# Perceiver block on one core: the place of the expert loop's preparation in the last rounds of a hand-ordered pipeline

## The chip, the core and the metric

The kernel is one program on one core of a Trainium2 chip. The metric is the device time of one execution in microseconds (us), the median over several executions; one further execution was taken with the hardware profiler, and all rows of the trace come from that one.

## What is computed

The reference is one block of a network with batch 128, 32 rows of 512 numbers in each batch entry, and a context of 257 rows for each entry. Everything is float32.

```python
x = x + xattn(layernorm(x), ctx_1024, ...)    # self attention, cross attention to the context, relu layer
x = x + attn(layernorm(x), W_attn, W_proj)    # 16 heads, causal, softmax times a decay matrix
x = x + ffn(layernorm(x), index_b, index_t, ...)
```

The last line is the one that matters here. `ffn` gives every row a gated feed-forward ("shared") result. The rows that `index_b`, `index_t` name get, besides, the result of one of eight experts:

```python
sh = ln(silu(x @ sw1.T + sb1) * (x @ sw2.T + sb2)); shared_out = sh @ sw3.T + sb3
x_moe = x[index_b, index_t]
expert_scores = sigmoid(x_moe @ eg_w.T + eg_b);  top1_idx = argmax(expert_scores + exp_bias)
z = ln(silu(x_moe @ ew1[e].T + eb1) * (x_moe @ ew2[e].T + eb2))       # for every expert e
final_out = shared_out.at[index_b, index_t].set(shared_moe_out + expert_moe_out)
```

## The kernel before, in words

**Tiles and stages.** 4096 rows are cut into 32 tiles of 128 rows. A tile goes through some forty named units on each engine (PE, DVE, ACT, POOL, and SP for transfers): `project_out` ends the head attention and gives x2, the rows that enter the feed-forward part; `x2_norm` normalizes them; `turn_x2n`, `ffn_in`, `ffn_in_l` are the transposes and the first product; DVE's `ffn_in` adds the bias, ACT's `ffn_in` is a tanh, `silu` and `z_norm` make the gated, normalized row; `turn_z`, `ffn_out`, `ffn_out_l` transpose and multiply it; DVE's `ffn_out` adds bias and x2, and SP stores the rows. Products are split in a float16 high part (line 1453) and a remainder (line 1462). What PE needs between these steps is written by ACT (lines 688, 696) and POOL (584).

**What sets the order.** Each engine runs its instructions strictly in the order in which the program issues them, and that order is written out by hand. `run_pipeline` goes through 37 rounds; in each it walks the engine's list of (lag, unit), and a unit of lag g works in round n on tile n - g. Three sets of lists exist: FIRST, ORDER and, for rounds 30 to 36, LAST. Between engines only semaphores order the work. In LAST there are also `keep_clock` units, which multiply the identity matrix into a bank that nobody reads (line 1594) and act on tile 31 alone.

**After the tiles** comes the expert loop. A list of the tiles with named rows is made from the indices; the loop runs once for each such tile (here once). Every turn reads the tile's x2 back from a scratch in HBM, normalizes it, transposes it (`turn_expert_rows`), multiplies it with the 9 gate columns (`gate_logits`), and for each of 8 experts does: product to 512 columns (`expert_in(k)`, line 1587), bias (line 1270), silu (line 796), norm, scaling by the choice (line 1304), transposes (line 1646) and the second product (line 1655). DVE begins a turn with a short chain on the logits, lines 1273 to 1291, which yields the coefficients, and only then adds the bias of expert 0.

**The units of this change.** The preparation for the loop's first turn stands in the pipeline, and acts on tile 31 alone:

```python
def first_rows(s, r, tile):            # DVE
    if tile == FINAL:
        dve.wait_ge(e_x2_loaded, 16)   # x2 of the first listed tile is back from HBM
        expert_moments(step, x2[:])    # lines 1215 to 1218
        dve.wait_ge(e_rstd_ready, 1)   # from POOL, line 600
        nc.vector.tensor_scalar(e_xn[:], x2[:], ...).then_inc(xn_ready, 1)   # line 1233
def first_rows(s, r, tile):            # PE: transposes (line 1575), then the gate products (line 1581)
        turn_expert_rows(1); gate_logits(1)
def first_expert(s, r, tile):          # PE: expert 0's first product (line 1587)
        expert_in(0)
```

ACT's `first_rows` copies the transposed rows out of PSUM (line 775), between PE's two steps; POOL's is the power that gives 1/std (line 600). On SP, `store_x2` (line 460) writes a tile's x2 to the scratch, and `first_x2` (line 508) waits until the stores of all tiles have landed and then reads the first listed tile. SP's list is the same in both kernels.

Of the kernel before, what the change touches and what calls it, by code (L numbers as in the profile page):

```python
# [121 lines left out]
        (2, "turn_x2n"), (1, "out_norm"), (1, "turn_x1n")],  # L122
}
LAST = {
    "pe": [(3, "ffn_out"), (3, "ffn_out_l"), (3, "first_rows"), (3, "first_expert"), (2, "project_q_l"),
        (1, "context_mix"), (2, "head_scores"), (2, "keep_clock0"), (0, "turn_xn"), (2, "project_v"),
        (0, "project_self"), (1, "turn_w"), (1, "keep_clock4"), (0, "project_self_l"), (1, "context_out"),
        (1, "keep_clock5"), (2, "project_v_l"), (2, "keep_clock2"), (0, "self_scores"), (0, "value_self"),
        (0, "value_self_l"), (0, "turn_p"), (2, "head_mix"), (2, "keep_clock1"), (1, "turn_h2"), (0, "self_mix"),
        (2, "project_out"), (2, "project_out_l"), (2, "keep_clock3"), (1, "hidden"), (1, "hidden_l"), (0, "turn_h"),  # L130
        (2, "turn_x2n"), (2, "keep_clock6"), (0, "project_query"), (0, "project_query_l"), (2, "ffn_in"),
        (0, "context_scores"), (2, "ffn_in_l"), (2, "keep_clock7"), (1, "turn_x1n"), (1, "project_k"),
        (1, "project_q"), (2, "turn_z"), (1, "project_k_l"), (0, "turn_pc")],
    "dve": [(3, "x2_norm"), (2, "hidden"), (2, "out_norm"), (2, "x1_norm"), (3, "ffn_in"), (3, "silu"),
        (1, "context_scores"), (3, "z_norm"), (3, "first_rows"), (2, "project_k"), (3, "ffn_out"), (0, "xn_moments"),
        (0, "turn_xn"), (2, "head_scores"), (1, "context_mix"), (1, "context_total"), (2, "head_total"),
        (2, "head_weights"), (0, "project_self"), (1, "context_out"), (0, "self_scores"), (1, "context_norm"),
        (0, "self_mix"), (2, "project_out"), (0, "self_norm")],
    "act": [(3, "turn_x2n_t"), (2, "turn_x1n"), (3, "ffn_in"), (2, "turn_x1n_t"), (1, "context_scores"),
        (3, "turn_z"), (3, "turn_z_t"), (3, "first_rows"), (1, "turn_pc"), (2, "project_k"), (2, "project_q"),  # L140
        (0, "turn_xn"), (0, "turn_xn_t"), (2, "head_scores"), (1, "turn_w"), (2, "project_v"), (0, "self_scores"),
        (0, "value_self"), (0, "turn_p"), (2, "head_mix"), (2, "head_mix_t"), (1, "turn_h2_t"), (1, "turn_h2"),
        (0, "turn_h"), (0, "turn_h_t"), (2, "turn_x2n"), (0, "project_query")],
    "pool": [(3, "silu"), (3, "first_rows"), (3, "turn_z"), (0, "xn_moments"), (0, "turn_xn"), (2, "head_scores"),
        (1, "context_out"), (2, "head_mix"), (0, "self_mix"), (1, "turn_h2"), (2, "project_out"), (0, "turn_h"),
        (1, "hidden"), (2, "turn_x2n"), (1, "out_norm"), (1, "turn_x1n")],
}
# [1581 lines left out]
```

## Time and profile before

| | |
|---|---|
| median of 3 runs | 1496.43 us (1494.0 to 1496.84) |
| the profiled execution | 1495.49 us, of which span 1493.6 us |
| mean granted TensorE clock | 0.987 of full speed |
| busy: PE, DVE, ACT, POOL | 1401.0, 1101.4, 530.6, 480.4 us |

The span is the time from the first to the last instruction of the trace; 1.9 us lie around it. The busy share is an average: the part that the change touches is the last 70 us of the span, in which tiles 30 and 31 drain out of the pipeline and the loop follows.

### The profile page before, as it was taken

To read this page: it belongs to the slowest core of one execution; us is meant where nothing else is said; L and a number is where in the kernel's file an instruction comes from. 1 tells how busy PE (TensorE), PEld (TensorE's weight loads), DVE (VectorE), ACT (ScalarE), POOL (GpSimd) and SP (SyncE) were. 2 spreads that over 40 slices of the span, in tenths; PEclk is the share of its full clock that TensorE was granted. 3 is DMA by queue.
4 is the path that set the end of the run, shared out by engine and by line. 5 is a ranking of instruction groups with operands and counts; after the bars stand their busy time and mean duration, and the time that the engine had idled before them with its cause. 6 is when DMAs were issued, how large, how long until landed. Compare 5 with 4: busy or idle time off the path is not lost.

```text
span 1493.6 us, 32437 instructions
## 1 busy us (share of the span) xinstructions
PE 1401.0 (94%) x13668; PEld 883.8 (59%) x13668; DVE 1101.4 (74%) x2215; ACT 530.6 (36%) x979; POOL 480.4 (32%) x499
## 2 busy tenths in 40 slices
PE   7779999999999999999999999999999999999789
PEld 3346666666565666666666566666656666665444
DVE  6667777777777777787777777777777777777645
ACT  2533333334333333333333333333433333343221
POOL 0033333333333333333333333333333333333211
PEclk9899999999999999999999999999999999999899
DMA  9632344333233344433323234444323324434530
GB/s 349 251 119 79 135 142 142 142 141 125 96 129 110 110 142 142 142 142 137 107 109 131 97 131 142 142 142 142 130 97 123 117 104 142 142 135 163 190 108 22
DMA packets 38657, 201.37 MB, mean 135 GB/s; under 512 B 5096, under 2 KB 5992, under 8 KB 28400
## 3 DMA queue, kind: packets, MB, share of 16 engines
q1 hardware_dynamic: 37792, 199.19, 37.2%
q8 instruction: 108, 1.77, 0.5%
q14 instruction: 37, 0.30, 0.1%
q10 hardware_dynamic: 720, 0.10, 0.0%
HBM read 182.24 MB, written 17.04 MB: 133 GB/s over the span
## 4 chain that ended last, share of the span: by engine, by line
PE 60%; DVE 22%; issue 9%; POOL 4%; ACT 3%; DMA 1%; SPq 0%; DVEq 0%; POOLq 0%; ACTq 0%
PE ps_a L1476 8%; PE ps_a L1442 8%; PE ps_t L1476 7%; PE ps_t L1434 6%; DVE stats L1005 4%; PE ps_a L1453 4%; PE ps_a L1517 4%; PE ps_a L1488 4%; POOL rstd L575 4%; PE ps_t L1453 4%; PE ps_v L1453 3%; DVE kbd L1126 3%; PE ps_a L1462 2%; PE ps_t L1488 2%; PE ps_a L1498 2%
## 5 line engine op out<-in xcount | busy, mean ns | idle before, releaser
L575 POOL TENSOR_TENSOR rstd<-var,mhalf 128x1 f32<-128x1 f32 x224 | 183.9, 821 | 444.2 <-DVE var L1007 444.0
L584 POOL TENSOR_TENSOR act_l<-act_t,act_h 128x512 f16<-128x512 f32 (+1 forms) x154 | 171.1, 1111 | 349.6 <-ACT act_t L696 261.1
L688 ACT ACTIVATE act_h<-ps_t,scale 128x512 f16<-128x512 f32 (+1 forms) x110 | 71.1, 646 | 176.7 <-PE ps_t L1434 176.7
L584 POOL TENSOR_TENSOR last_slot<-last_slot 128x512 f16<-128x512 f32 (+1 forms) x70 | 77.4, 1106 | 153.6 <-ACT last_slot L696 114.1
L1126 DVE TENSOR_SCALAR kbd<-ps_a,unscale 32x512 f32<-32x512 f32 x64 | 48.2, 754 | 54.9 <-PE ps_a L1488 53.8
L1442 PE MATMUL ps_a<-wcv,act_t 128*128 128x512 f32 x176 | 82.1, 610 | 2.2 <-ACT act_t L702 2.2
L1005 DVE BATCH_NORM_STATS2 stats<-rows 128x6 f32<-128x512 f32 x110 | 76.4, 695 | 3.8
L1434 PE MATMUL ps_t<-ident,rows 128*128 128x128 f32 x352 | 57.4, 286 | 19.7 <-DVE rows L1011 19.5
L696 ACT ACTIVATE act_t<-ps_t,scale 128x512 f32<-128x512 f32 (+1 forms) x110 | 70.3, 639 | 0.2 <-PE ps_t L1434 0.2
L1453 PE MATMUL ps_a<-w_parts,act_h 128*128 128x512 f16 x264 | 65.0, 383 | 1.3 <-ACT act_h L688 1.3
L1166 DVE STREAM_TRANSPOSE pbd<-rows 32x512 f32<-32x512 f32 x88 | 61.8, 703 | 2.8
L1434 PEld LDWEIGHTS ps_t<-ident,rows 128*128 128x128 f32 x352 | 39.2, 142 | 41.6 <-DVE rows L1011 32.9
L1533 PE MATMUL ps_a<-ctx_n,p_t 128*32 128x512 f32 x512 | 63.3, 613 | 0.5 <-ACT p_t L730 0.5
L1054 DVE SCALAR_TENSOR_TENSOR rows<-ps_t,inv,rows 128x512 f32<-128x512 f32 x22 | 16.5, 751 | 63.1 <-PE ps_t L1509 32.6
L1476 PE MATMUL ps_a<-act_h,wattn 128*128 128x128 f16 x704 | 46.1, 227 | 17.3 <-ACT act_h L688 17.3
L1018 DVE SCALAR_TENSOR_TENSOR rows<-rows,rstd,beta 128x512 f32<-128x512 f32 x66 | 50.8, 770 | 12.2 <-POOL rstd L575 12.2
L688 ACT ACTIVATE last_slot<-ps_t,scale 128x512 f16<-128x512 f32 (+1 forms) x50 | 32.3, 646 | 69.2 <-PE ps_t L1434 69.2
L1476 PEld LDWEIGHTS ps_a<-act_h,wattn 128*128 128x128 f16 x704 | 42.3, 102 | 22.6 <-ACT act_h L688 21.5
L1442 PEld LDWEIGHTS ps_a<-wcv,act_t 128*128 128x128 f32 x176 | 32.3, 194 | 35.0 <-issue 35.0
L688 ACT ACTIVATE act_h<-ps_a,scale 128x512 f16<-128x512 f32 x22 | 15.1, 687 | 104.8 <-PE ps_a L1434 104.8
L751 ACT ACTIVATE v_n<-ps_v,unscale 128x512 f32<-128x512 f32 x22 | 15.1, 687 | 99.6 <-PE ps_v L1462 99.6
L1014 DVE SCALAR_TENSOR_TENSOR rows<-rows,mv,gamma 128x512 f32<-128x512 f32 x66 | 49.0, 742 | 0.0
(369 smaller groups left out, 3291.8 us busy)
## 6 DMA issues: line engine op xcount, KB each, us to landing
ctx_t<-in_ctx_t SPq DMA_DIRECT2D x32, 2056.0 KB, 8.1
ctx_n<-in_ctx_n SPq DMA_DIRECT2D x32, 2048.0 KB
ctx_last<-in_ctx_last SPq DMA_DIRECT2D x32, 256.0 KB
x_in<-in_x SPq DMA_DIRECT2D x22, 256.0 KB, 7.2
x_scratch<-rows SPq DMA_DIRECT2D x22, 256.0 KB, 8.7
out<-rows SPq DMA_DIRECT2D x22, 256.0 KB, 2.0
wattn<-in_ew SPq DMA_DIRECT2D x6, 512.0 KB, 5.6
out<-last_slot SPq DMA_DIRECT2D x11, 256.0 KB, 2.0
```

The lines of the kernel that those rows point to most:

```text
L575: nc.gpsimd.tensor_tensor(rstd[s][:], var[s][:], mhalf[:], ALU.pow).then_inc(rstd_ready[s], 1)
L584: nc.gpsimd.tensor_tensor(act_l[s][:, chunks], act_t[s][:, chunks], act_h[s][:, chunks], ALU.subtract).then_inc(act_l_ready[s], 1)
L688: nc.scalar.activation(act_h[s][:, 0:width // P].rearrange("p c r -> p (c r)"), bank[s][:, 0:width], ACT.Copy, scale=scale[:, k:k + 1]).th ...
L696: nc.scalar.activation(act_t[s][:, 0:width // P].rearrange("p c r -> p (c r)"), bank[s][:, 0:width], ACT.Copy, scale=scale[:, k:k + 1]).th ...
L1005: chain(nc.vector.bn_stats(stats[s][:], rows))
L1126: nc.vector.tensor_scalar(kbd[rows, :, :, h, :], ps_a[s][rows, :].rearrange("p (c g k) -> p c g k", c=C, g=G), unscale[rows, K_WATTN:K_WAT ...
L1434: mm = nc.tensor.transpose(out[s][:, c * P:(c + 1) * P], rows[s][:, lo + c * P:lo + (c + 1) * P], ident[:])
L1442: mm = nc.tensor.matmul(out, left[:, c, :], w[:, c, :], start=(c == 0), stop=(c == C - 1))
L1453: nc.tensor.matmul(bank[s][:], act_h[s][:, c, :], w[:, part, c, lo:lo + D], start=(c == 0 and part == 0), stop=False, skip_group_check=True)
L1476: nc.tensor.matmul(bank[s][:, m * P:(m + 1) * P], w[:, part, c, lo + m * P:lo + (m + 1) * P], act_h[s][:, c, :], start=(m == 0 and c == 0 ...
L1488: mm = nc.tensor.matmul(bank[s][:, m * P:(m + 1) * P], w[:, 0, c, lo + m * P:lo + (m + 1) * P], act_l[s][:, c, :], start=False, stop=(c == ...
L1533: mm = nc.tensor.matmul(ps_a[s][T * g:T * (g + 1), :], p_t[s][:, c * P + T * g:c * P + T * (g + 1)], ctx_n[:, g, c, :], start=(c == 0), st ...
```

## The change

In the four lists of LAST, `first_rows` moves ahead of the work of tile 31's own gate. On PE `first_rows` and `first_expert` stood behind `ffn_out_l` of tile 31 and now stand ahead of `turn_z` of tile 31, in the round before (lag 2). On DVE `first_rows` stood behind `z_norm` and now stands ahead of `ffn_in`; on ACT it moves from behind `turn_z_t` to ahead of `turn_z`; on POOL from behind `silu` to ahead of it. No instruction is added, dropped or altered. The lists' lines with these entries:

```diff
 LAST = {
-    "pe": [(3, "ffn_out"), (3, "ffn_out_l"), (3, "first_rows"), (3, "first_expert"), (2, "project_q_l"),
...
+        (2, "keep_clock7"), (1, "turn_x1n"), (1, "project_k"), (1, "project_q"), (2, "first_rows"),
+        (2, "first_expert"), (2, "turn_z"), (1, "project_k_l"), (0, "turn_pc")],
...
+    "dve": [(3, "x2_norm"), (2, "hidden"), (2, "out_norm"), (2, "x1_norm"), (3, "first_rows"), (3, "ffn_in"),
...
-        (3, "turn_z"), (3, "turn_z_t"), (3, "first_rows"), (1, "turn_pc"), (2, "project_k"), (2, "project_q"),
+        (3, "first_rows"), (3, "turn_z"), (3, "turn_z_t"), (1, "turn_pc"), (2, "project_k"), (2, "project_q"),
...
-    "pool": [(3, "silu"), (3, "first_rows"), (3, "turn_z"), (0, "xn_moments"), (0, "turn_xn"), (2, "head_scores"),
+    "pool": [(3, "first_rows"), (3, "silu"), (3, "turn_z"), (0, "xn_moments"), (0, "turn_xn"), (2, "head_scores"),
```

On DVE, behind `x2_norm` of tile 31 (L1011), the order was and is as follows; `last_slot` is here the buffer into which x2 of the listed tile is read back, L1183 and L1187 are `ffn_in` of tile 31.

```order
 L1007 TENSOR_SCALAR var<-mv 128x1
 L1011 TENSOR_SCALAR rows<-rows,mv,rstd 128x512
+L1215 BN_STATS stats<-last_slot 128x6
+L1217 BN_AGGR mv<-stats 128x2
+L1218 TENSOR_SCALAR var<-mv 128x1
+L1233 TENSOR_SCALAR last_slot<-last_slot,mv,rstd 128x512
 L1183 SCALAR_TENSOR_TENSOR rows<-ps_a,unscale,b 128x512
 L1187 SCALAR_TENSOR_TENSOR v_n<-rows 128x256
```

So the four instructions of `first_rows` come ahead of tile 31's `ffn_in`. They are taken from DVE's place between `z_norm` (L1018) and `ffn_out` (L1206, L1208) of tile 31:

```order
 L1014 SCALAR_TENSOR_TENSOR v_n<-v_n,mv,ln_g 128x256
 L1018 SCALAR_TENSOR_TENSOR v_n<-v_n,rstd,ln_b 128x256
-L1215 BN_STATS stats<-last_slot 128x6
-L1217 BN_AGGR mv<-stats 128x2
-L1218 TENSOR_SCALAR var<-mv 128x1
-L1233 TENSOR_SCALAR last_slot<-last_slot,mv,rstd 128x512
 L1206 SCALAR_TENSOR_TENSOR rows<-ps_a,unscale,b 128x512
 L1208 TENSOR_TENSOR rows<-rows 128x512
```

Behind them nothing else moved on DVE. On PE, from the end of tile 31's `ffn_in_l` (L1462) to the loop's head (L392), with `turn_z` (L1434 from v_n) and `ffn_out` (L1453, L1462) of tile 31:

```order
 L1462 MATMUL ps_a<-w_parts,act_l 128x512 x4
 L1594 MATMUL ps_e<-ident 128x128 x4
-L1434 MATMUL ps_t<-ident,v_n 128x128 x2
-L1453 MATMUL ps_a<-w_parts,act_h 128x512 x4
-L1462 MATMUL ps_a<-w_parts,act_l 128x512 x2
 L1575 MATMUL ps_t<-ident,last_slot 128x128 x4
 L1581 MATMUL ps_e<-beta,last_slot 128x9 x4
 L1587 MATMUL ps_a<-wqk,last_slot 128x512 x4
+L1434 MATMUL ps_t<-ident,v_n 128x128 x2
+L1453 MATMUL ps_a<-w_parts,act_h 128x512 x4
+L1462 MATMUL ps_a<-w_parts,act_l 128x512 x2
 L392 TENSOR_LOAD redo
```

Tile 31's three steps now stand behind all three steps of the loop's preparation, the product of expert 0 among them.

## Rows read from the trace of the kernel before

**Rows 1.** Page, part 1: busy us (share of the span) and instructions of each engine
```profile
PE 1401.0 (94%) x13668; PEld 883.8 (59%) x13668; DVE 1101.4 (74%) x2215; ACT 530.6 (36%) x979; POOL 480.4 (32%) x499
```

**Rows 2.** Transfers 1415:1450: issues, median us to landing; SP's timeline
```profile
x_scratch<-rows SPq DMA_DIRECT2D x1, 256.0 KB, 4.3
last_slot<-x_scratch SPq DMA_DIRECT2D x1, 256.0 KB, 2.6
1424.29 0.34 SPq L460 DMA_DIRECT2D x_scratch<-rows  x1
1429.73 0.36 SPq L508 DMA_DIRECT2D last_slot<-x_scratch  x1
```

**Rows 3.** Timeline 1426:1441: start, duration, engine, line, operation, [idle before <-releaser]
```profile
1426.06 0.55 DVE L1011 TENSOR_SCALAR rows<-rows,mv,rstd 128x512 f32<-128x512 f32 x1 [0.67 <-POOL rstd L575]
1426.66 0.66 PE L1434 MATMUL ps_t<-ident,rows 128*128 128x128 f32 x4 [2.30 <-DVE rows L1011]
...
1430.85 1.05 PE L1594 MATMUL ps_e<-ident 128*128 128x128 f32 x8
1431.05 0.75 DVE L1183 SCALAR_TENSOR_TENSOR rows<-ps_a,unscale,b 128x512 f32<-128x512 f32 x1 [4.44 <-PE ps_a L1462]
1431.83 0.42 ACT L770 ACTIVATE v_n<-rows 128x256 f32<-128x256 f32 x1 [3.21 <-DVE rows L1183]
1434.56 0.48 DVE L1018 SCALAR_TENSOR_TENSOR v_n<-v_n,rstd,ln_b 128x256 f32<-128x256 f32 x1 [0.52 <-POOL rstd L575]
1434.96 0.69 DVE L1215 BATCH_NORM_STATS2 stats<-last_slot 128x6 f32<-128x512 f32 x1
1435.10 0.62 PE L1434 MATMUL ps_t<-ident,v_n 128*128 128x128 f32 x2 [3.20 <-DVE v_n L1018]
1436.84 0.88 DVE L1233 TENSOR_SCALAR last_slot<-last_slot,mv,rstd 128x512 f32<-128x512 f32 x1 [0.66 <-POOL rstd L600]
1438.94 0.75 DVE L1206 SCALAR_TENSOR_TENSOR rows<-ps_a,unscale,b 128x512 f32<-128x512 f32 x1 [1.22 <-PE ps_a L1462]
1439.37 0.58 ACT L775 COPY last_slot<-ps_t 128x512 f32<-128x512 f32 x1 [2.77 <-PE ps_t L1575]
1439.72 0.69 DVE L1208 TENSOR_TENSOR rows<-rows 128x512 f32<-128x512 f32 x1
1440.10 1.03 PE L1581 MATMUL ps_e<-beta,last_slot 128*128 128x9 f32 x8 [0.77 <-ACT last_slot L775]
```

**Rows 4.** Timeline 1441:1450, the loop's first microseconds
```profile
1441.60 0.17 DVE L1273 TENSOR_TENSOR logits<-ps_e,beta 128x9 f32<-128x9 f32 x1 [1.19 <-PE ps_e L1581]
1448.55 1.12 PE L1642 MATMUL ps_v<-b,coef_t 8*128 8x512 f32 x2 [0.34 <-ACT coef_t L808]
1448.87 0.35 DVE L1304 TENSOR_SCALAR p_n<-p_n,pick 128x256 f32<-128x256 f32 x1
1449.61 0.44 PE L1646 MATMUL ps_t<-ident,p_n 128*128 128x128 f32 x2
1449.88 3.60 PE L1587 MATMUL ps_a<-wcqk,last_slot 128*128 128x512 f32 x8
```

**Rows 5.** Windows 1460:1470: busy us of PE, PEld, DVE, ACT, POOL; granted clock, DMA
```profile
1460.00:1470.00 10.00, 10.00 (x28) 4.64 (x27) 6.64 (x18) 1.38 (x4) 1.44 (x2) 1.00 0.17 52
```

**Rows 6.** Timeline around 1280, an earlier tile's step from turn_z to ffn_out
```profile
1278.71 0.39 PE L1434 MATMUL ps_t<-ident,v_n 128*128 128x128 f32 x2
1281.61 0.75 DVE L1206 SCALAR_TENSOR_TENSOR rows<-ps_a,unscale,b 128x512 f32<-128x512 f32 x1
```

**Rows 7.** Windows of 1 us, PE alone: busy us, granted clock, DMA share, GB/s
```profile
1414.00:1415.00 1.00, 0.00 (x0) 0.87 1.01 406
1421.00:1422.00 1.00, 1.00 (x4) 0.72 1.12 207
1435.00:1436.00 1.00, 0.62 (x2) 0.61 0.00 0
1438.00:1439.00 1.00, 1.00 (x6) 0.68 0.00 0
```

More of the change, by code:

```diff
@@ L124 @@
 LAST = {
-    "pe": [(3, "ffn_out"), (3, "ffn_out_l"), (3, "first_rows"), (3, "first_expert"), (2, "project_q_l"),
[L126 to L133, printed above, removed]
@@ L134 @@
-    "dve": [(3, "x2_norm"), (2, "hidden"), (2, "out_norm"), (2, "x1_norm"), (3, "ffn_in"), (3, "silu"),
-        (1, "context_scores"), (3, "z_norm"), (3, "first_rows"), (2, "project_k"), (3, "ffn_out"), (0, "xn_moments"),
+    "pe": [(3, "ffn_out"), (3, "ffn_out_l"), (2, "project_q_l"), (1, "context_mix"), (2, "head_scores"),
+        (2, "keep_clock0"), (0, "turn_xn"), (2, "project_v"), (0, "project_self"), (1, "turn_w"), (1, "keep_clock4"),
+        (0, "project_self_l"), (1, "context_out"), (1, "keep_clock5"), (2, "project_v_l"), (2, "keep_clock2"),
+        (0, "self_scores"), (0, "value_self"), (0, "value_self_l"), (0, "turn_p"), (2, "head_mix"),
+        (2, "keep_clock1"), (1, "turn_h2"), (0, "self_mix"), (2, "project_out"), (2, "project_out_l"),
+        (2, "keep_clock3"), (1, "hidden"), (1, "hidden_l"), (0, "turn_h"), (2, "turn_x2n"), (2, "keep_clock6"),
+        (0, "project_query"), (0, "project_query_l"), (2, "ffn_in"), (0, "context_scores"), (2, "ffn_in_l"),
+        (2, "keep_clock7"), (1, "turn_x1n"), (1, "project_k"), (1, "project_q"), (2, "first_rows"),
+        (2, "first_expert"), (2, "turn_z"), (1, "project_k_l"), (0, "turn_pc")],
@@ L136 @@
+    "dve": [(3, "x2_norm"), (2, "hidden"), (2, "out_norm"), (2, "x1_norm"), (3, "first_rows"), (3, "ffn_in"),
+        (3, "silu"), (1, "context_scores"), (3, "z_norm"), (2, "project_k"), (3, "ffn_out"), (0, "xn_moments"),
         (0, "turn_xn"), (2, "head_scores"), (1, "context_mix"), (1, "context_total"), (2, "head_total"),
```

## The prediction

> **What bounds the kernel now.** I read the page first. PE is busy 94% of the span, DVE 74% [rows 1], so the body of the kernel is PE's. The change, however, touches only the end, where tiles 30 and 31 drain. There I read the timeline of all engines from 1405 us on, then the transfers, then the granted clock in windows of 1 us, and last the loop.
>
> The reader is to see four things. First, from 1431.90 (the end of the clock-keeping product, 1430.85 + 1.05) to 1435.10 PE waits 3.20 us for tile 31's gate [rows 3]: tile 31 is alone in the pipeline, and its chain runs from engine to engine. Second, that chain ends on DVE: ffn_in starts at 1431.05, z_norm ends at 1434.56 + 0.48 = 1435.04, ffn_out runs from 1438.94 to 1440.41, and the loop's logits start at 1441.60 [rows 3, 4]. The gate products that they need had ended at 1440.10 + 1.03 = 1441.13, 0.47 us earlier, so the start was not set by PE alone; DVE loads the tile list and its register in this place. Third, from 1440.41 the first scaled z (L1304) is ready at 1448.87 + 0.35 = 1449.22, 8.81 us later, and PE turns it at 1449.61 [rows 4]. From there PE is busy without a gap (10.00 of 10.00 us at full clock [rows 5]) to the end. So whatever moves PE's 1449.61 moves the end of the kernel by as much. Fourth, the rows that the preparation needs come late: the store of x2 of tile 31 is issued at 1424.29 and takes 4.3 us, to 1428.6; SP waits for it, loads the tile's number, issues the read at 1429.73, and the read takes 2.6 us [rows 2]. They are there at about **1432.33**. Before, DVE came to them at 1434.96, with 2.6 us to spare.
>
> **The change part by part.** It removes and adds no instruction; all of it is a matter of who waits for whom. SP's order stands, so 1432.33 stays.
>
> *DVE.* It now comes to the preparation after x2_norm, at about 1426.7, and has to wait for the read until 1432.33, say 1432.40 with the wake-up. Behind it in the queue stands tile 31's ffn_in, whose product is ready at 1431.05, and behind that everything that PE, ACT and POOL do for tile 31. From the start of L1215 to the start of L1233 it takes 1436.84 - 1434.96 = 1.88 us, POOL's power included. L1233 took 0.88 us beside a POOL subtraction, which is no longer near it; the row's own 0.88 is the upper bound, and the same kind of instruction at 1426.06, of 0.55 us, is what I take. So xn is ready at 1432.40 + 1.88 + 0.55 = 1434.83, and ffn_in starts there instead of at 1431.05: **+3.8 us**. The next steps of the gate are unchanged (3.99 us from 1431.05 to 1435.04), so z_norm ends at about 1438.85 instead of 1435.04 [rows 3].
>
> *PE.* It turns the rows at 1434.87 (0.66 us, like the four at 1426.66). ACT's order has tile 31's tanh ahead of the copy: the tanh can start 0.78 us after ffn_in does (1431.83 against 1431.05), at 1435.61, takes 0.42, and the copy 0.58: done at 1436.65 [rows 3]. Then 1.03 us of gate products and 3.60 us of the product of expert 0 [rows 3, 4], at full clock to X = 1441.3. Tile 31's z has been ready since 1438.85 and stands behind it: 2.5 us more. turn_z to DVE's ffn_out took 1438.94 - 1435.10 = 3.84 us here and 1281.61 - 1278.71 = 2.90 us with an earlier tile [rows 3, 6]. The difference is the clock (below), and I take 2.90. DVE's ffn_out takes 1.47. So it ends at E = X + 4.37 = 1445.7 instead of 1440.41.
>
> *The loop's head.* From E it takes DVE 8.81 us to the scaled z, as before: the logits wait for DVE's own loads, and expert 0's product, now long done, had not held the bias up in a way that I can use. PE turns z then at once, E + 8.86, where before it came 0.39 us late because of the product L1642 in front of it, which now is done earlier. That is all that the early product gives back: 0.33 us. PE: 1454.5 against 1449.61, **+4.9 us** at full clock.
>
> *The clock, first place.* In rows: the granted clock fell at 1435.22 (0.61 in that microsecond, so 22% of it at full) and was back at 1438.64, 3.4 us at the lower of its two levels, 1.2 GHz; ahead of the fall PE had waited 3.20 us. At 1414.74 it fell, again while PE waited (no PE work in that microsecond), and was back at 1421.56, after 6.8 us [rows 7]. Now PE's wait is 1431.90 to 1434.87, about as long, so the fall at 1435.2 should come again. Bound below: back after 3.4 us, which slows only 0.9 us of work, +0.5. Bound above: back after 6.8 us, at 1442.0, which slows all of the expert's product, +2.2. The work that follows the fall is now broken by a wait for ACT, like that after 1414.74, and not a solid run as at 1436: I take +2.2, in all **+7.1**.
>
> *The clock, second place.* After ffn_out_l PE has one product left, expert 1's, 3.6 us, to about X + 7.4. Scaled z comes at X + 13.2. In between are only a transpose of 8 columns and L1642 (1.12 us). Before, expert 0's product filled this hole. So I expect a second fall here. It costs half of the time that PE then works at 1.2 GHz: below 0 (no fall), above 3.4 (6.8 us of work). Some of the slow stretch passes while PE still waits; I take **1.2**.
>
> Sum: 4.9 + 2.2 + 1.2 = **+8.3 us**. Against the profiled execution that is 1495.49 + 8.3 = 1503.8; the median of the runs shown is 0.94 higher, 1496.43, and so the forecast for a median is 1504.7.
>
> The read's price is where a rule bears. The rows give 2.6 us for the read and 4.3 us for the store, which stood behind the loads of the biases and expert weights. The Trainium skill, DMA: Bandwidth & Descriptors, section "Anatomy of one DMA", gives a fixed 2.0 us and bytes over 436 GB/s (a fit for the GpSimd path). As an estimate from that page, 256 KB take 2.6 us either way; the read agrees, the store does not, and by the page the rows would be back 1.7 us sooner and the sum 6.6. The same page, section "Rules for kernel authors",, says to issue a transfer early and wait on it late, which speaks against this change: it moves the wait 8 us forward and leaves the issue where it was. The trace's 2.6 us to spare agrees.
>
> **What else moves.** The store of tile 31's rows (SP, L464) and the read of the old rows behind it go later by the delay of E; the loop uses the old rows after expert 2, more than 10 us on. ACT and POOL wait with DVE and have no other work. Expected cost nothing.
>
> **The rivals.**
> - *A: slower, but the clock is kind.* The same waits, with neither long stretch at 1.2 GHz: +4.9 to +5.9, 1501.3 to 1502.3. For it: two clock-keeping products still stand ahead of the wait, and after a wait of 2.30 us, at 1426.66, four transposes took 0.66 us, where two took 0.62 at 1435.10 with the clock down [rows 3]. Against: the 3.2 us wait here did drop it. 0.25.
> - *B: slower still.* Both stretches long, and DVE's L1233 0.88: 7.1 + 3.4 + 0.3 = +10.8, 1507.2. 0.15.
> - *C: not slower.* The rows would be back before 1431.05 - 2.43 = 1428.6, so that DVE does the preparation inside its 4.44 us wait for PE and ffn_in is not late. That decides from 1428.6 on, and each microsecond later costs one until z waits for expert 0's product. Even then that product, behind the turn, ACT's copy and the gate products, would end at about 1438.1, turn_z would start there instead of at 1435.10, and the sum would be +3.0 - 0.94 - 0.33 = +1.7: 1498.1, within 0.2%. Against it: the read was issued only at 1429.73. 0.07.
> - *D: faster.* PE's queue at the loop's head is shorter by the turn, the gate products and 3.6 us of expert 0. If the loop's first z were waiting for PE, up to 3.7 us would be won and the wait of 3.2 us filled. The rows give PE 0.39 us there, no more; it would need DVE's 8.81 us to shrink. 1492.7. 0.03.
>
> **How the numbers follow.** The forecast has 0.50. 0.2% is 3.0 us, about what a measurement of this kernel can tell from no change. The forecast, A and B are all slower by more: 0.90. C is no change, and I count 0.01 of D there too, for a part of its gain: same 0.08, faster 0.02. The range takes in A with 1.3 us below it for the spread of the runs, and B with 1.8 above it: 1500 to 1509.
>
> **What would show it.** In the changed trace: DVE's L1215 starts near 1432.4 after an idle of some 5.7 us that a transfer ended; L1183 near 1434.8; PE waits from 1431.9 to 1434.9 for L1233; L1434 from v_n starts right behind L1587, near 1443.5 (1441.3 if the clock is kind), and not behind DVE; DVE's L1208 ends near 1447.9; the first L1646 near 1456.7, after a PE wait for DVE; and the clock is below 1.00 in windows near 1436 to 1442 and near 1452 to 1459. Wrong would be: L1215 without a wait (C), L1434 waiting for DVE's L1018 (the product is no hindrance), or PE busy up to L1646 (D).

## The result, and the profile after

The changed kernel takes 1505.6 us (median of 4, 1504.03 to 1506.82) against 1495.78 us (median of 4, one run more than in the table ahead of the prediction) for the kernel before: ratio 1.0066, 95% interval 1.0049 to 1.0084, so **9.9 us slower** (7.3 to 12.6). The forecast was 8.3 us slower, 1504.7, in a range of 1500 to 1509.

The timeline of the changed kernel, columns as in [rows 3]. The whole trace runs 1.1 us later than that of before already ahead of the change (L1172, tile 31's project_out on DVE, starts at 1424.65 instead of 1423.51), so I compare distances and not absolute times.

```profile
1424.65 0.75 DVE L1172 SCALAR_TENSOR_TENSOR rows<-ps_a,unscale,rows 128x512 f32<-128x512 f32 x1 [7.51 <-PE ps_a L1462]
...
1433.90 0.69 DVE L1215 BATCH_NORM_STATS2 stats<-last_slot 128x6 f32<-128x512 f32 x1 [6.14 <-DMA last_slot<-x_scratch]
...
1435.78 0.55 DVE L1233 TENSOR_SCALAR last_slot<-last_slot,mv,rstd 128x512 f32<-128x512 f32 x1 [0.67 <-POOL rstd L600]
1436.24 0.74 DVE L1183 SCALAR_TENSOR_TENSOR rows<-ps_a,unscale,b 128x512 f32<-128x512 f32 x1
1436.38 1.08 PE L1575 MATMUL ps_t<-ident,last_slot 128*128 128x128 f32 x4 [3.33 <-DVE last_slot L1233]
...
1438.22 1.85 PE L1581 MATMUL ps_e<-beta,last_slot 128*128 128x9 f32 x8 [0.77 <-ACT last_slot L775]
...
1439.74 0.48 DVE L1018 SCALAR_TENSOR_TENSOR v_n<-v_n,rstd,ln_b 128x256 f32<-128x256 f32 x1 [0.52 <-POOL rstd L575]
1439.92 5.34 PE L1587 MATMUL ps_a<-wqk,last_slot 128*128 128x512 f32 x8
1445.10 0.38 PE L1434 MATMUL ps_t<-ident,v_n 128*128 128x128 f32 x2
...
1447.87 0.75 DVE L1206 SCALAR_TENSOR_TENSOR rows<-ps_a,unscale,b 128x512 f32<-128x512 f32 x1 [7.64 <-PE ps_a L1462]
...
1450.54 0.17 DVE L1273 TENSOR_TENSOR logits<-ps_e,beta 128x9 f32<-128x9 f32 x1 [1.19 <-issue]
...
1457.81 0.35 DVE L1304 TENSOR_SCALAR p_n<-p_n,pick 128x256 f32<-128x256 f32 x1
...
1458.22 0.69 PE L1646 MATMUL ps_t<-ident,p_n 128*128 128x128 f32 x2 [1.89 <-DVE p_n L1304]
```

Read it from the top. DVE waits 6.14 us for the read of x2. Tile 31's ffn_in (L1183) follows only then. Its z is ready at 1440.22, but PE turns it (L1434) at 1445.10 and behind nothing but its own queue: the row has no idle in front. In between stands L1587, expert 0's product, of 5.34 us. The logits start 1.19 us after ffn_out, to the hundredth the same as before [rows 4], and now the row says "issue", with PE's gate products done at 1440.07, 10 us earlier. In this place DVE loads the loop's count and the tile's number into registers (two TENSOR_LOADs, of 0.56 and 0.33 us in the trace of before); they, and not the gate products, set that start in both kernels. The last row has a PE wait of 1.89 us for DVE; before, PE had no idle there [rows 4].

The granted clock, in windows of all engines of the changed kernel (length; busy us of PE, PEld, DVE, ACT, POOL; granted clock; DMA share; GB/s):

```profile
1436.00:1444.00 8.00, 6.85 (x18) 4.27 (x19) 3.47 (x9) 1.00 (x2) 0.72 (x1) 0.57 0.01 2
1452.00:1456.00 4.00, 1.23 (x4) 0.38 (x3) 2.66 (x10) 2.14 (x5) 0.00 (x0) 1.00 0.24 68
1456.00:1464.00 8.00, 6.11 (x10) 2.70 (x10) 4.59 (x13) 0.69 (x2) 1.44 (x2) 0.57 0.00 0
1464.00:1470.00 6.00, 6.00 (x16) 2.64 (x15) 2.51 (x7) 0.69 (x2) 0.72 (x1) 1.00 0.00 0
```

Twice in 30 us it is mostly at 1.2 GHz. The first time it slows the gate products and expert 0's product. The second time follows 4 us in which PE was busy for 1.23. In windows of 1 us that fall lies at 1456.9 (0.97 in the microsecond from 1456) and the return at 1463.8; PE works from 1458.22 on, so 5.5 of these 6.8 us are work of the loop's body, and half of 5.5 is 2.8 us.

**Where the time is.** Ahead of the change there is a mark that all kernels share: SP's issue of the late expert weights (L470). From there I measure four points, each the difference of two times in one trace: the end of z_norm, the start of turn_z (L1434 from v_n), PE's turning of the first scaled z of the loop (L1646), and the end of the span. "Rest" is the span's end minus the first z. The time against the kernel before is from the ratio of the runs; its interval is in brackets.

| kernel | z_norm ends | turn_z | first z | span ends | rest | against before, us |
|---|---|---|---|---|---|---|
| before | 23.18 | 23.24 | 37.75 | 81.74 | 43.99 | |
| the change | 27.30 | 32.18 | 45.30 | 92.08 | 46.78 | +9.9 (7.3 to 12.6) |
| e1 | 27.46 | 27.52 | 46.18 | 91.48 | 45.30 | +7.9 (5.7 to 10.3) |
| e2 | 23.42 | 35.24 | 48.35 | 95.00 | 46.65 | +13.6 (11.1 to 16.0) |
| e3 | 27.68 | 27.74 | 42.12 | 86.17 | 44.05 | +5.1 (3.1 to 6.9) |
| e4 | 23.21 | 25.67 | 38.95 | 85.40 | 46.45 | +4.0 (2.5 to 5.5) |
| e5 | 23.38 | 23.44 | 37.95 | 82.02 | 44.07 | -0.6 (-2.1 to 0.7) |
| e6 | 27.72 | 29.94 | 43.05 | 88.39 | 45.34 | +7.0 (4.6 to 9.6) |
| e7 | 23.34 | 23.40 | 35.64 | 79.93 | 44.29 | -2.5 (-3.9 to -1.0) |
| e8 | 28.90 | 28.96 | 43.55 | 89.02 | 45.47 | +5.5 (3.4 to 7.6) |
| e9 | 24.90 | 28.83 | 41.94 | 88.82 | 46.88 | +6.9 (4.6 to 9.3) |
| e10 | 28.35 | 34.55 | 47.67 | 91.70 | 44.03 | +6.6 (4.2 to 8.8) |
| e11 | 23.16 | 23.22 | 34.37 | 78.58 | 44.21 | -3.4 (-4.9 to -1.9) |

For the change: 4.1 us at z_norm, 8.9 at turn_z, 7.6 at the first z, 10.3 at the end. The rest differs by 2.8.

Two things limit the table. Each row is one profile, and in the timed runs only e3, e4, e5, e7 and e11 have intervals that lie clear of the change's; where two intervals overlap (e1, e2, e6, e8, e9 and e10 with the change), the profiles have to tell the kernels apart. And in e1 and e3 the fall of the clock that the kernel before has at 1414.7 came only at 1426.0 and 1423.3, so x2 of tile 31 was ready 2.5 us sooner after the mark. Their z_norm is not touched by it, because DVE waits for the read in both.

### The profile page after: what moved, and what is told of

The parts are those of the page before. It is cut to its first block, busy times and chain, and to the rows that moved or that the text cites. A ratio compares the mean times of both kernels' runs of the same rounds, so it can differ in the third digit from the quotient of the medians.

```text
span 1505.0 us, 32437 instructions
## 1 busy us (share of the span) xinstructions
PE 1406.9 (93%) x13668; PEld 886.5 (59%) x13668; DVE 1101.4 (73%) x2215; ACT 531.1 (35%) x979; POOL 480.9 (32%) x499
## 4 chain that ended last, share of the span: by engine, by line
PE 60%; DVE 22%; issue 10%; POOL 4%; ACT 3%; DMA 1%; SPq 0%; POOLq 0%; DVEq 0%; ACTq 0%
PE ps_a L1476 8%; PE ps_a L1442 8%; PE ps_t L1476 7%; PE ps_t L1434 5%; DVE stats L1005 4%; PE ps_a L1517 4%; PE ps_a L1453 4%; PE ps_a L1488 4%; POOL rstd L575 4%; PE ps_t L1453 4%; PE ps_v L1453 3%; DVE kbd L1126 3%; PE ps_t L1488 2%; PE ps_a L1462 2%; PE ps_a L1498 2%
## 5 line engine op out<-in xcount | busy, mean ns | idle before, releaser
L1434 PE MATMUL ps_t<-ident,rows 128*128 128x128 f32 x352 | 57.4, 286 | 19.7 <-DVE rows L1011 19.5
L1453 PE MATMUL ps_a<-w_parts,act_h 128*128 128x512 f16 x264 | 64.2, 379 | 1.3 <-ACT act_h L688 1.3
L1434 PEld LDWEIGHTS ps_t<-ident,rows 128*128 128x128 f32 x352 | 39.2, 142 | 41.6 <-DVE rows L1011 32.9
L1018 DVE SCALAR_TENSOR_TENSOR rows<-rows,rstd,beta 128x512 f32<-128x512 f32 x66 | 50.8, 770 | 12.3 <-POOL rstd L575 12.3
```

The lines of the kernel that those rows point to most:

```text
L1434: mm = nc.tensor.transpose(out[s][:, c * P:(c + 1) * P], rows[s][:, lo + c * P:lo + (c + 1) * P], ident[:])
L1453: nc.tensor.matmul(bank[s][:], act_h[s][:, c, :], w[:, part, c, lo:lo + D], start=(c == 0 and part == 0), stop=False, skip_group_check=True)
```

## The experiments

The theory after the result: **two waits in a row** (DVE for the read of x2, then tile 31's z behind expert 0's product on PE) and **two falls of the clock** that they bring. The rivals: the read's wait alone; the order on PE alone; no part for the clock.

### e1_vector_half: DVE and POOL early, PE and ACT as before

```diff
-    "dve": [..., (2, "x1_norm"), (3, "ffn_in"), (3, "silu"), ..., (3, "z_norm"), (3, "first_rows"),
+    "dve": [..., (2, "x1_norm"), (3, "first_rows"), (3, "ffn_in"), (3, "silu"), ..., (3, "z_norm"),
-    "pool": [(3, "silu"), (3, "first_rows"), (3, "turn_z"),
+    "pool": [(3, "first_rows"), (3, "silu"), (3, "turn_z"),
```

> Only DVE and POOL do the preparation early; PE and ACT keep the order of before. My theory: two waits add up in the change, DVE's for the read of x2 (about 4 us, from the trace of the changed kernel) and tile 31's z behind expert 0's product on PE. Here only the first is left: turn_z 4.0 us later after L1172 than before, and the kernel 4.0 us slower, up to 6 if the clock stays low longer. Rival 1, that the wait for the read is the whole cost: +10. Rival 2, that the read's wait is covered and PE's order is the whole cost: 0.

Measured: +7.9 us, more than expected; the size missed. turn_z is 4.3 us late, as the theory has it, but the first z 8.4. Granted clock of PE in e1 (columns: length, PE busy, clock, DMA share, GB/s):

```profile
1436.00:1440.00 4.00, 0.00 (x0) 0.52 0.00 0
1440.00:1446.00 6.00, 4.28 (x12) 0.50 0.00 0
1446.00:1453.00 7.00, 6.94 (x14) 0.50 0.24 76
1453.00:1454.00 1.00, 1.00 (x4) 0.87 0.00 0
```

PE had waited 8.55 us for z. The clock fell in that wait and stayed down for 17 us, through tile 31's last products and most of expert 0's. e8 tests this. The interval of e1 reaches to 10.3, so e1 alone does not rule out that the read's wait is the whole cost; e2 and e3 do.

### e2_tensor_half: PE and ACT early, DVE and POOL as before

```diff
-    "dve": [..., (3, "first_rows"), (3, "ffn_in"), (3, "silu"), (1, "context_scores"), (3, "z_norm"),
+    "dve": [..., (3, "ffn_in"), (3, "silu"), (1, "context_scores"), (3, "z_norm"), (3, "first_rows"),
-    "pool": [(3, "first_rows"), (3, "silu"), (3, "turn_z"),
+    "pool": [(3, "silu"), (3, "first_rows"), (3, "turn_z"),
```

(against the changed kernel)

> Only PE and ACT do the preparation early; DVE and POOL keep the order of before, so no engine waits for the read. My theory: xn is ready 14.2 us after the start of L1172 as before, then turn, copy, gate products and expert 0's product stand ahead of turn_z, which starts 20 us (full clock) to 23 us (1.2 GHz) after L1172, against 11.6 before and 20.5 in the change. So +10 to +13 us against before, no better than the whole change, although the wait for the read is gone. Rival 1, that the wait for the read is the whole cost: 0.

Measured: +13.6 us. z_norm ends as before (23.42), no engine waits for the read, and turn_z is 12 us late. The rival that the read's wait is the whole cost is out. With e1, the two halves are no sum: 7.9 + 13.6 is far over 9.9. In the whole change the early DVE half lets PE's half begin sooner: PE turns the rows 23.5 us after the mark, in e2 25.8.

The rest of e2, 46.65, is two falls of the clock. The one at the loop's head was half as long as in the change (down from 1457.4 to 1460.9, PE at work from 1458.05, so 1.4 us), and one more came behind expert 7 (1.3 us; see e6):

```profile
1457.00:1461.00 4.00, 2.95 (x6) 1.51 (x7) 2.72 (x8) 0.69 (x2) 0.10 (x2) 0.57 0.00 0
```

### e3_expert_late: the change with expert 0's product back behind ffn_out_l

```diff
-        (2, "keep_clock7"), ..., (2, "first_rows"), (2, "first_expert"), (2, "turn_z"), ...
+        (2, "keep_clock7"), ..., (2, "first_rows"), (2, "turn_z"), ...
-    "pe": [(3, "ffn_out"), (3, "ffn_out_l"), (2, "project_q_l"),
+    "pe": [(3, "ffn_out"), (3, "ffn_out_l"), (3, "first_expert"), (2, "project_q_l"),
```

> The changed kernel with expert 0's product back behind ffn_out_l; turns and gate products stay early. My theory: the gate products end before z is ready, so turn_z starts 4.0 us later than before, not 8.9; the hole at the loop's head is filled again, so the second fall of the clock goes too. +3.7 us against before, up to +5. If the early product were not what costs beyond the read's wait: +9 to +10 as in the change. If only the clock did: +7.

Measured: +5.1 us, at the upper end of what was expected. turn_z follows z_norm at once, 4.5 us late; the rest is 44.05, as before.

```profile
1438.17 0.69 PE L1434 MATMUL ps_t<-ident,v_n 128*128 128x128 f32 x2 [0.18 <-DVE v_n L1018]
```

So the early product costs the change some 5 us: 4.8 between the timed runs, and 5.9 in the profiles, of which 3.2 stand at the first z (4.4 at turn_z) and 2.7 are the second fall. The first fall was there in e3 too, from 1433.7 to 1443.9, and cost nothing: from the end of z_norm to the first z it took 14.44 us, 14.57 before.

### e6_clock_held: the change with identity products in PE's waits

```diff
+                def hold_clock(n):
+                    for c in range(n):
+                        nc.tensor.matmul(ps_z[:, 2 * P:3 * P], ident[:], ident[:], start=True, stop=True)
+                        hold_clock(12)
                         turn_expert_rows(1)
+                        hold_clock(3)
                         pe.wait_ge(small_loaded, 16 * 7)
...
                     expert_in(1)
+                    hold_clock(7)
                     pe.wait_ge(coef_ready, i + 1)
...
+                    hold_clock(4)
                     pe.wait_ge(coef_t_ready, i + 1)
...
+                    hold_clock(6)
                     for k in range(NE):
```

> The changed kernel with 12 identity products put into PE's wait ahead of the turns (3.1 us), 3 into the wait for ACT's copy, and 6, 4 and 6 into the three waits at the loop's head, all into a bank nobody reads. My theory: the two falls of the clock cost 3.0 us (turns, gate products and expert 0 at 1.2 GHz) and 2.8 us (the loop after its first z) in the change; with both held off it is 4.4 to 5 us slower than before and not 10. If the clock has no part in it: +10, or more by what the added products delay.

(As run, it has 7 products in the first wait of the loop's head, not 6.) Measured: +7.0, not 4.4 to 5. The clock was held in the places meant (1.00 in every window from 1423 to 1493): turn_z is 2.2 us sooner than in the change, the first z 2.3, and 5.3 late in all. From the turn of the rows to turn_z it took 6.07 us, against 8.72 (1436.38 to 1445.10) in the change:

```profile
1435.78 0.66 PE L1575 MATMUL ps_t<-ident,last_slot 128*128 128x128 f32 x4 [0.88 <-DVE last_slot L1233]
1441.85 0.38 PE L1434 MATMUL ps_t<-ident,v_n 128*128 128x128 f32 x2
```

But the rest is 45.34. The last two products of the timeline show why:

```profile
1492.89 2.90 PE L1664 MATMUL ps_v<-wattn,p_t 128*128 128x512 f32 x4 [0.46 <-ACT p_t L811]
1495.59 4.42 PE L1587 MATMUL ps_a<-wqk,last_slot 128*128 128x512 f32 x8
```

In the kernel after the change they are

```profile
1498.88 1.98 PE L1655 MATMUL ps_v<-wattn,p_t 128*128 128x512 f32 x4 [0.46 <-ACT p_t L811]
1500.70 3.60 PE L1587 MATMUL ps_a<-wqk,last_slot 128*128 128x512 f32 x8
```

The clock fell once more, behind the short waits for expert 7's z, and cost 1.3 us. It did so in the profiles of e1, e2, e6 and e8, not in those of before, the change, e3, e4, e5, e7, e9 and e10, with the same work and waits in that place. What decides it no run shows.

### e8_vector_half_held: e1 with 30 and 3 identity products in PE's waits

```diff
+        (1, "project_q"), (2, "hold_for_z"), (2, "turn_z"), ...
+                def hold_for_z(s, r, tile):
+                    if tile == FINAL:
+                        hold_clock(30)
                         turn_expert_rows(1)
+                        hold_clock(3)
```

> e1_vector_half with 30 identity products (about 7.9 us) in PE's wait ahead of turn_z and 3 in the wait for ACT's copy. In e1 the first scaled z was turned 8.4 us later than before, of which 4.3 stood already at the end of z_norm; the rest is the granted clock, at 1.2 GHz for 17 us from the wait of 8.6 us on. If so, with the clock held the first z is turned 3.4 to 4.4 us later than before and the kernel is about 4 us slower, up to 5.5 if the last wait of the kernel drops the clock. If the rest was another wait and not the clock: 8 us slower as e1.

Measured: +5.5 us; e1 and e8 overlap in their intervals, so it is the profiles that tell them apart. From the end of z_norm to the first z it takes 14.57 us before, 18.72 in e1, 14.65 in e8. So e1's extra 4.2 us are the clock. (In e8 it fell too, but only from 1441.7 to 1445.1, and that cost nothing.) (That the first z is 5.8 late and not the expected 3.4 to 4.4 comes ahead of z_norm: in this execution DVE waited 7.56 us for a read that took 4.1.)

### e4_own_rows_after and e5_own_rows_before: no wait for the read

```diff
-                        dve.wait_ge(e_x2_loaded, 16)
-                        expert_moments(step, x2[:])
+                        own = rows3[s_last]
+                        expert_moments(step, own[:])
...
-                        nc.vector.tensor_scalar(e_xn[:], x2[:], ...
+                        nc.vector.tensor_scalar(e_xn[:], own[:], ...
...
                 dve.wait_ge(bias_loaded, 16 * NE)
+                dve.wait_ge(e_x2_loaded, 16)
```

e4 is this in the changed order, e5 in the order of before.

> The changed order, but DVE's first_rows norms x2 of tile 31 where it lies in SBUF (the first listed tile of these indices) and does not wait for the read; the read is waited for ahead of the loop. This is rival C of the prediction made real. My theory: DVE's wait is gone and so is PE's long wait, the clock stays up, and what is left is tile 31's z behind expert 0's product: +1.5 us against before (turn_z 2.8 us later, 0.94 won back by the clock, 0.33 at the first z), up to +2.8 with the clock's fall in the last wait. If the order alone were the cost, read or no read: +6 or more. If the early product were a gain once the rows are there: below 0.

> Control: the order of before with the same first_rows from SBUF. The read had 2.6 us to spare in that order, so nothing should move: 0, within 1 us. If the read's landing held the kernel before: faster by up to 1.

e5: -0.6 (-2.1 to 0.7), no difference, as expected. e4: +4.0 us. z_norm ends where it did before, turn_z is 2.4 us late, the first z 1.2 (1.5 expected): rival C's mechanism as worked out. The sum missed, because the rest is 46.45. The clock of e4 (all engines):

```profile
1446.00:1450.00 4.00, 1.06 (x4) 0.38 (x3) 2.72 (x10) 2.14 (x5) 0.00 (x0) 1.00 0.21 68
1450.00:1458.00 8.00, 6.12 (x11) 2.65 (x10) 4.65 (x14) 0.69 (x2) 1.44 (x2) 0.57 0.00 0
1458.00:1462.00 4.00, 4.00 (x12) 1.89 (x11) 1.32 (x3) 0.69 (x2) 0.00 (x0) 1.00 0.00 0
```

The early product leaves its hole at the loop's head whether the rows are late or not, and the second fall comes with it, 2.5 us. I had left that out of rival C. Against the change, e4 shows the price of the read's wait with the first fall that followed it: 9.9 - 4.0 = 5.9 us, with intervals that do not overlap.

### e10_loop_head_held: the change with only the loop's head held

```diff
                     expert_in(1)
+                    hold_clock(6)
...
+                    hold_clock(4)
                     pe.wait_ge(coef_t_ready, i + 1)
...
+                    hold_clock(6)
                     for k in range(NE):
```

> The changed kernel with identity products only in the three waits of the loop's head (6, 4 and 6). My theory: it removes only the second fall of the clock, which cost 2.8 us from the first z to the end in the profile of the change: about 7.3 us slower than before, up to 8.6 with a fall in the last wait. If the holes cost nothing: 10.

Measured: +6.6 us against 9.9 in the change, 7.3 expected; the intervals overlap. The profile is the evidence: the rest is 44.03 against 46.78, so the second fall is 2.75 us, and gone. (The profiled execution as a whole was hardly shorter than the change's, 91.70 against 92.08 from the mark: its first z was 2.4 us later. Of these, 1.05 stood at z_norm, and 1.3 are the first fall, which lasted 10.2 us here and 6.8 in the change, so that expert 0's product took 6.63 us and not 5.34.)

### e9_biases_after_read: SP loads the experts' biases behind the read of x2

```diff
+                def late_biases(s, r, tile):
+                    if tile == FINAL:
                         sp.wait_ge(scored[s], 3 * r + 3)
                         for e in range(NE):
...
-         (3, "store_x2"), (3, "first_x2"),
+         (3, "store_x2"), (3, "first_x2"), (3, "late_biases"),
```

> The changed kernel, with SP issuing the eight loads of the experts' biases behind the read of x2 and not ahead of the store. My theory: the store of x2 takes 4.6 us to land because it stands behind 2 MB of biases; without them it takes 2.0 to 2.6 us, the read is issued and lands about 2 us sooner, DVE waits about 4 us and not 6.1, and everything up to the first z is 2 us sooner: 8 us slower than before and not 10. If the store is slow by itself, or the clock decides alone: 10 as in the change.

Measured: +6.9 us. The transfers of the changed kernel, and those of e9 (KB each, median us to landing), and DVE's wait in e9:

```profile
x_scratch<-rows SPq DMA_DIRECT2D x1, 256.0 KB, 4.6
last_slot<-x_scratch SPq DMA_DIRECT2D x1, 256.0 KB, 2.7
```

```profile
x_scratch<-rows SPq DMA_DIRECT2D x1, 256.0 KB, 2.0
last_slot<-x_scratch SPq DMA_DIRECT2D x1, 256.0 KB, 2.8
```

```profile
1428.86 0.70 DVE L1218 BATCH_NORM_STATS2 stats<-last_slot 128x6 f32<-128x512 f32 x1 [3.65 <-DMA last_slot<-x_scratch]
```

The store lands in 2.0 us instead of 4.6, DVE waits 3.65 and not 6.14, z_norm ends 2.4 us sooner, and turn_z and the first z come 3.35 us sooner. The read's lateness is thus a real term of the change, and 2.6 us of it come from the 2 MB that stand ahead of the store. 2 us were expected, 3.35 came in the profile and 3.0 between the timed runs (whose intervals overlap). The 0.95 us beyond z_norm are the clock: it fell only at 1434.0 here, behind the gate products, which took 1.03 us and not 1.85.

### e7_choice_early and e11_choice_early_held: a version drawn from the theory

The loop's head is DVE's: 8.81 us from ffn_out to the first scaled z. So what belongs in tile 31's waits is not expert 0's product but DVE's choice of the expert. Both versions rely on tile 31 being the first listed tile, as it is with these indices: they take its x2 from SBUF, as e4 does. In the pipeline, shortened:

```diff
-    "pe": [(3, "ffn_out"), (3, "ffn_out_l"), (3, "first_rows"), (3, "first_expert"), ...
+    "pe": [(3, "ffn_out"), (3, "ffn_out_l"), (3, "first_expert"), ...
+        (2, "ffn_in_l"), (2, "first_rows"), (2, "keep_clock7"), (2, "first_gate"), ... (2, "turn_z"), ...
+    "dve": [(3, "x2_norm"), ... (3, "first_rows"), (3, "ffn_in"), (3, "silu"), (1, "context_scores"),
+        (3, "first_logits"), (3, "z_norm"), (3, "first_choice"), ... (3, "ffn_out"), ...
+    "act": [... (3, "first_rows"), (3, "turn_z"), (3, "turn_z_t"), (3, "first_shares"), ...
...
+                def first_choice(s, r, tile):
+                    if tile == FINAL:
+                        choice_of(first_step, 0, sel[:, FINAL:FINAL + 1])
...
+                    logits_of(i + 1)                # at the end of a turn of the loop, for the next one
+                    choice_of(step, i + 1, sel[:, bass.ds(tile_of(dve, i + 1), 1)])
```

`logits_of` and `choice_of` are lines 1273 to 1291, which no longer stand at the head. e11 adds `hold_clock(4)` behind the gate products and 4 and 3 ahead of the last two waits of the loop.

> A version drawn from the theory: rows from SBUF as in e4 (it relies on tile 31 being the first listed one), turns and gate products ahead of turn_z as in the change, expert 0's product behind ffn_out_l as before, and DVE's and ACT's choice of the expert (L1273 to L1291), which stood in the 8.8 us from ffn_out to the first scaled z, taken out of the loop's head into tile 31's waits; in the loop it stands at the end of a turn for the next one. ffn_out ends 0.9 us earlier with the clock kept, and expert 0's product, not DVE, then sets the bias: first z turned 3.7 us earlier than before, kernel 3 to 4 us faster. If the head of the loop was not bound by DVE's chain: 0 to -1.

> e7_choice_early with 4 identity products in PE's wait ahead of tile 31's turn_z and 4 and 3 in the last two waits of the loop. e7's first z was turned 2.1 us earlier than before instead of the 3.7 expected, with the clock down from ahead of turn_z to ffn_out_l (0.94 us and the start of expert 0's product). If that is the missing part, the first z comes 3 us earlier than before and the kernel is 3 to 3.5 us faster; if the added products change nothing, 2.5 as e7.

e7: -2.5 us, less than the 3 to 4 expected; the first z is 2.1 us early and not 3.7. Its windows from 1433 to 1438, and the stretch of e11 with the same work:

```profile
1433.00:1438.00 5.00, 4.26 (x11) 1.99 (x12) 3.11 (x14) 2.42 (x5) 0.67 (x1) 0.66 0.00 0
```

```profile
1436.00:1441.00 5.00, 4.26 (x14) 1.95 (x15) 3.41 (x13) 2.42 (x5) 0.67 (x1) 1.00 0.00 0
```

With four more products ahead of turn_z the clock stays at 1.00, the first z is 3.4 us early and the kernel -3.4 us (-4.9 to -1.9): 1491.53 us against 1495.3. It is faster than both kernels. e7's and e11's intervals overlap; the 1.3 us between their first z are the profiles'.

## Why the prediction was right

- **x2 comes late, and DVE waits for it.** Right. L1215 was to start 8.89 us after L1172 (1432.40 against 1423.51) and started 9.25 after it, 6.14 us idle and ended by the transfer. ffn_in was to be 3.8 us late and z_norm as much; z_norm is 4.1 late. e9 shows the wait to be a cause: take 2.6 us off the store, and z_norm comes 2.4 us sooner. e4 takes the wait away whole, and z_norm ends where it did before.
- **z stands behind expert 0's product.** Right: 2.5 us at full clock and 2.2 more for the clock were forecast, 4.9 came (1440.22 to 1445.10), and e3 takes it away. That the two agree so well is in part luck, as the next point shows. e2 shows that the product costs without any wait for the read.
- **The clock, first place.** Right in place, and the long stretch was the right choice of the two: down from 1436.5 to 1443.3, 6.8 us. The choice itself was lucky: the fall in PE's wait for the rows lasted 10.2 us in e2, e3 and e10, and 3.4 in e9, where it came a little later. The sum was wrong on the way. The products took 1.08, 1.85 and 5.34 us instead of 0.66, 1.03 and 3.60, 3.0 in all; the turns' 0.42 were hidden, because ACT copied the rows only after its tanh, which ended at 1437.44. Against e6 the clock cost 8.72 - 6.07 = 2.65 us, forecast 2.2; at full clock the way takes 6.07 us, forecast 6.43. The two errors cancel. Both bounds of the prediction, 0.5 and 2.2, are too small by its own rule (half of the time at 1.2 GHz in which PE works): from 1436.65 to 1438.64 and to 1442.0 that gives 1.0 and 2.7.
- **What the early product gives back at the loop's head.** Right: 8.81 us again, and 9.2 from ffn_out to the first z of before became 8.87 (1449.35 to 1458.22).
- **The clock, second place.** Right that it falls, wrong in size: the term was 1.2 us, and the rest grew by 2.8 (e10: 2.75). The sentence "Some of the slow stretch passes while PE still waits" was the fault. The clock fell only at 1456.9, 1.3 us ahead of the first z, and 5.5 of its 6.8 us were PE work. Half of PE's work in the stretch is the price in all four profiles that have this fall: 2.8 in the change and in e9, 2.5 in e4, and 1.4 in e2, where the stretch was 3.4 us long. Of the 2.0 us between the forecast 8.3 and the 10.3 in the profile, 1.6 are this, 0.3 the read's wait (4.1 at z_norm and not 3.8) and 0.1 what lies between.
- **Rival A** (the clock is kind) is out by the trace. **Rival B** was nearer with its 3.4 us for the second fall (2.8 measured) than the 1.2 that I took; its 0.88 us for L1233 did not come (0.55). **Rival C** had its mechanism right (e4: turn_z 2.4 late, first z 1.2) and its sum wrong, +4.0 for +1.7, by the second fall. **Rival D** is out: the loop's first z waits for DVE, and only moving DVE's chain (e7, e11) gained.
- **The rule on fixed cost.** The Trainium skill, DMA: Bandwidth & Descriptors, section "Anatomy of one DMA", would have put the store at 2.6 us, an estimate from a fit that the page gives for the GpSimd path, while these transfers are SP's. With the biases out of the way it took 2.0 (e9), with them 4.6: the estimate is 0.6 us off in the first case, and the loads ahead of the store make the second.

Open: what decides whether the clock falls in a given wait, and for how long; and whether the wait for the read would be as long if the kernel had more than one listed tile, or another one first; no run changed the indices.

## What to carry to other kernels

Preparation moved ahead of a chain that is alone on all engines is not free because PE idles there: ask which input it waits for, when that landed, and what stands behind it in each in-order queue. Then look at the hole that it leaves: here expert 0's product had covered the choice on DVE, and without it the clock fell and cost 2.8 us, against 4.1 for the read's wait. If a loop's head is bound by one engine's small chain, move that chain into the idle time, not the big product of the engine that is waiting.

## What the runs showed of the hardware that I had not expected

- The landing of a small transfer was set by the queue, not by its issue. With the biases ahead of it, the store of x2 landed 16.7 to 18.2 us after the mark (the issue of L470), whether it was issued 12.5 us after the mark, as in most kernels (it then took 4.2 to 5.6 us), or 9.9, as in e1 and e3 (7.2 and 7.6 us). In e9, without the biases, it landed at 14.6 and took 2.0. The read itself took 2.6 to 2.8 us, in e6, e7 and e11 3.0, in e8 4.1.
- Whether the clock falls at a given short wait, and for how long, differs between profiles with the same work in that place. The last two products of the kernel took 1.98 and 3.60 us, or, in e6, 2.90 and 4.42, which moved the end by 1.3 us. PE's wait for the rows or for z brought 3.4 us at 1.2 GHz before, 6.8 in the change, 10.2 in e2, e3 and e10, 17 in e1. This may be a part of the spread between runs of one kernel (1497.43 to 1506.23 in e1); no kernel has two profiles that would show it.
- Matmuls with 9 columns feel the clock too: L1581 took 1.03 us at full clock and 1.85 at 1.2 GHz.
